# Six gather buffers and later matrix products in the three middle stages of a graph network kernel

## The reference

```
# layer 1
scale = norm(h[src]) * norm(h[dst]) + 1e-6           # norms over all edges
c     = relu((h[src] * h[dst] / scale) @ proj_cosim)
gate  = exp(clip(c.sum(-1), -5, 5))
diff  = segment_sum(h[src] - h[dst], dst)            # per node
out   = relu(segment_sum(diff[src] * gate, dst) @ W_ffn.T + b_ffn)
# layer 2
agg   = segment_sum(h[src], dst)
out   = relu((h + agg) @ W0 + b0) @ W1 + b1
```

## Time and profile before

| what | value |
|---|---|
| median of 3 runs | 5672.16 us (5667.63 to 5672.7) |
| profiled execution, span | 6105.6 us (its page gives no other time of its own) |
| PE busy | 4432.3 us (73%) |
| DVE busy | 4412.9 us (72%) |
| POOL busy | 3619.2 us (59%) |
| ACT busy | 2446.8 us (40%) |
| mean granted TensorE clock | 0.784 of full speed |

### The profile page before, as it was taken

The page is one execution under the profiler, slowest core; times in us unless marked ns, Lnnn a source line. Parts: engine busy times, 40 slices in busy tenths (PEclk is TensorE's granted clock), DMA queues, the critical chain, the costliest instruction groups (busy, mean ns, idle before and its releaser), DMA issues. The chain is left out here.

```text
span 6105.6 us, 72124 instructions
## 1 busy us (share of the span) xinstructions
PE 4432.3 (73%) x17616; PEld 2513.0 (41%) x17681; DVE 4412.9 (72%) x7837; ACT 2446.8 (40%) x7859; POOL 3619.2 (59%) x3943
## 2 busy tenths in 40 slices
PE   0577776679999986999655546555787878777776
PEld 0455554534444434666444432222333334344443
DVE  5678787768888878999766656555666766666665
ACT  0567776624434432555433322211222333333333
POOL 1556655466666640000267668776777667777776
PEclk9888898889999998999755555555778866767776
DMA  9233234433434337999533324444555522222221
GB/s 360 100 103 105 100 117 131 131 76 84 88 82 88 86 71 200 285 286 287 165 87 86 85 75 108 105 103 99 135 144 143 140 76 65 66 65 61 64 63 37
DMA packets 833422, 725.15 MB, mean 119 GB/s; under 512 B 535904, under 2 KB 543010, under 8 KB 832880
## 3 DMA queue, kind: packets, MB, share of 16 engines
q1 hardware_dynamic: 534000, 513.27, 28.9%
q0 software_dynamic: 101440, 90.01, 8.3%
q10 hardware_dynamic: 197568, 117.25, 6.2%
HBM read 450.28 MB, written 273.76 MB: 119 GB/s over the span
## 5 line engine op out<-in xcount | busy, mean ns | idle before, releaser
L1382 POOL DMA_INDIRECT df_hs<-u,keep_idx x392 | 419.1, 1069 | 879.5 <-POOLq L243 701.9
L802 POOL DMA_INDIRECT t<-keep_ptr_pay,keep_scat_ptr x392 | 410.0, 1046 | 390.6 <-DVE den_df L659 138.3
L896 POOL DMA_INDIRECT sc_xg<-t,keep_gather x392 | 435.8, 1112 | 329.3 <-DVE sc_h L196 175.2
L1382 POOL DMA_INDIRECT hd_gat<-u,keep_idx x392 | 475.5, 1213 | 158.8 <-issue 116.5
L1909 POOL DMA_INDIRECT out_x<-hd_x,keep_scat_out x392 | 453.3, 1156 | 143.3 <-issue 118.5
L1382 POOL DMA_INDIRECT ml_gat<-u,keep_idx x392 | 399.8, 1020 | 158.9 <-issue 93.5
L1382 POOL DMA_INDIRECT pr_gat<-sd,keep_idxsd x392 | 408.6, 1042 | 137.1 <-issue 69.9
L1543 PE MATMUL df_ps_p<-keep_weights,df_prod 64*128 64x64 f32 x784 | 189.8, 421 | 271.7 <-ACT df_junk_p L1526 156.4
L1065 PE MATMUL sc_ps_r<-sc_qx,keep_weights 128*64 128x512 f32 x784 | 359.4, 601 | 31.3 <-DVE sc_prod L977 28.1
L1371 PE MATMUL at_ps_m<-at_vx,keep_msg_twice 128*128 128x512 f32 x784 | 361.7, 605 | 22.6 <-DVE at_vx L1262 22.6
L2049 PE MATMUL hd_ps_h<-keep_weights,hd_xb 128*128 128x128 f32 x784 | 245.7, 413 | 145.3 <-DVE hd_wn L1992 119.9
(11 more groups left out here) (313 smaller groups left out, 12478.9 us busy)
## 6 DMA issues: line engine op xcount, KB each, us to landing
u<-den_dh SPq DMA_DIRECT2D x196, 256.0 KB
t<-tab_row ACTq DMA_DIRECT2D x98, 272.0 KB, 11.3
tab_x<-in_x SPq DMA_DIRECT2D x98, 256.0 KB
den_dx<-in_x SPq DMA_DIRECT2D x98, 256.0 KB
out_x<-den_dx SPq DMA_DIRECT2D x98, 256.0 KB
sc_et<-in_etype_row SPq DMA_DIRECT2D x98, 256.0 KB
at_v<-vt SPq DMA_DIRECT2D x196, 128.0 KB
at_et<-in_etype_row SPq DMA_DIRECT2D x98, 256.0 KB
```

Source lines behind the costliest of these rows:

```text
L802: pool.indirect_dma_start(pairs, bass.IndirectOffsetOnAxis(ap=e.scat_ptr[:, c:c + 1], axis=0), e.ptr_pay[:, c, :], None, bounds_check=NP * ...
L896: pool.indirect_dma_start(xg[i][:, u, :], None, e.T0, bass.IndirectOffsetOnAxis(ap=e.gather0[:, b.n, u:u + 1], axis=0), bounds_check=NP - ...
L1382: pool.indirect_dma_start(gat[i][:, u, :], None, table, bass.IndirectOffsetOnAxis(ap=idx_all[:, c:c + 1], axis=0), bounds_check=rows - 1, ...
```

## The change

Only `difference`, `propagate`, `mlp` and `gather` are touched. The tiles that POOL gathers into get AHEAD = 6 places, all other rings W = 5 places, each with its own semaphores. The waits that guard a place move with them: POOL may be 6 groups ahead of its reader, not 3. PSUM: `difference` has T = 4 places of ps_t (3 before), `propagate` T = 3 for ps_t and ps_x as before and two places for ps_f (one before), `mlp` two places for hid (one before). The lags between engines grow:

| stage, what | before | after |
|---|---|---|
| difference: group that DVE reads in ps_t in step n | n-1 | n-2 |
| difference: product, transposed sd on PE; their readers on ACT | n-2; n-2 | n-3; n-3 |
| propagate: PE turn, W_ffn, transpose | n-1, n-3, n-5 | n-1, n-4, n-7 |
| propagate: DVE scan, add, norm; ACT relu | n-2, n-4, n-6; n-3 | n-3, n-6, n-9; n-5 |
| mlp: PE W0, W1, transpose, last turn, own rows, gathered rows | n-2, n-2, n-4, n-6, n, n | n-3, n-5, n-7, n-9, n-1, n |
| mlp: DVE scan, x3, norm; ACT relu, copy out | n-1, n-3, n-5; n-2, n-6 | n-2, n-6, n-8; n-4, n-10 |

`ps_p`, `ps_b`, `ps_1`, `ps_2`, `ps_o`, and the ps_x and last-turn tile of mlp stay single. The memset behind each gather is gone. The order on PE changes in `difference` (the turn of hs comes first) and in `mlp`.

The core of the diff:

```diff
+AHEAD = 6
+W = 5
...
-def gather(pool, table, idx_all, gat, gathered, st, pos, rows, rest=None, rested=None):
+def gather(pool, table, idx_all, gat, gathered, st, pos, rows):
...
-        if rest is not None:
-            wait(pool, rested, st.n * TU + u)
-            pool.memset(rest[:, :], 0.0).then_inc(rested, 1)
... difference
-        hs = [s.sb(f"hs{i}", [P, TU, D]) for i in range(U)]
+        hs = [s.sb(f"hs{i}", [P, TU, D]) for i in range(AHEAD)]
...
+        T = 4
+        ps_t = [s.ps(f"t{i}", [D, GE]) for i in range(T)]
...
-                    wait(pool, turned, st.n - (U - 1), e.pool_passed)
-                    wait(pool, sq1, st.n - (U - 1), e.pool_passed)
+                    wait(pool, turned, st.n - (AHEAD - 1), e.pool_passed)
+                    wait(pool, sq1, st.n - (AHEAD - 1), e.pool_passed)
...
-                    b = st.back(1)
+                    b = st.back(2)
                     if b.on():
                         v.wait_ge(turned, b.n + 1)
                         v.wait_ge(hb_done, b.n + 1)
-                        wait(v, p_ready, b.n - (U - 1))
+                        wait(v, p_ready, b.n - (W - 1))
...
-                    b = st.back(2)
+                    b = st.back(3)
+                    if st.on():
+                        r = st.ring(AHEAD)
+                        wait(pe, gathered[r.s], 16 * TU * (r.k + 1), e.pe_passed)
+                        wait(pe, sd_done, st.n - (T - 1), e.pe_passed)
+                        for u in range(TU):
+                            m = pe.transpose(ps_t[st.n % T][:, u * P:(u + 1) * P], hs[r.s][:, u, :], e.C["ident"])
+                        m.then_inc(turned, 1)
... propagate
-        ps_f = s.ps("f", [D, GE])
+        F = 2
+        ps_f = [s.ps(f"f{i}", [D, GE]) for i in range(F)]
...
-                    b, f, g = st.back(2), st.back(4), st.back(6)
+                    b, f, g = st.back(3), st.back(6), st.back(9)
...
-                    d, f, x = st.back(1), st.back(3), st.back(5)
+                    d, f, x = st.back(1), st.back(4), st.back(7)
...
-                        wait(pe, relu_done, f.n, e.pe_passed)
-                        pe.matmul(ps_f[:, :], e.W["ffnT"][0:D, :], agg[f.s][:, :], start=True, stop=True).then_inc(f_ready, 1)
+                        wait(pe, relu_done, f.n - (F - 1), e.pe_passed)
+                        pe.matmul(ps_f[f.n % F][:, :], e.W["ffnT"][0:D, :], agg[f.s][:, :], start=True, stop=True).then_inc(f_ready, 1)
... mlp
-                    d, x, t = st.back(2), st.back(4), st.back(6)
+                    o, d, f, x, t = st.back(1), st.back(3), st.back(5), st.back(7), st.back(9)
+                    if f.on():
+                        wait(pe, hid_done, f.n + 1, e.pe_passed)
+                        wait(pe, x3_done, f.n, e.pe_passed)
+                        pe.matmul(ps_2[:, :], e.W["w1"], hid[f.n % 2][:, :], start=True, stop=True).then_inc(h2_ready, 1)
```

More of the change, by code:

```diff
@@ L35 @@
 LAST = 2
-REST = 128
 EARLY = 48
@@ L84, in first, with ring @@
         return isinstance(self.n, int) and self.n == 0
+    def ring(self, size):
+        return Step(self.n, self.n // size, self.n % size, size)
 def run_groups(eng, body, u=U, tail=LAST):
@@ L1440, in body @@
                         sp.dma_start(edge_rows(e.SD, pos(b) * GE), sdr[b.s][:, :, :]).then_inc(sd_out[b.s], 16)
-                run_groups(sp, body, U, 4)
-                for i in range(U):
-                    wait(sp, sd_out[i], 16 * len(range(i, NG, U)), e.sp_passed)
+                run_groups(sp, body, W, 5)
+                for i in range(W):
+                    wait(sp, sd_out[i], 16 * len(range(i, NG, W)), e.sp_passed)
             @block.vector
@@ L1550, in body @@
                         m.then_inc(b_ready, 1)
-                    if st.on():
-                        i = st.s
-                        wait(pe, gathered[i], 16 * TU * (st.k + 1), e.pe_passed)
-                        wait(pe, sd_done, st.n - (U - 1), e.pe_passed)
-                        for u in range(TU):
-                            m = pe.transpose(ps_t[i][:, u * P:(u + 1) * P], hs[i][:, u, :], e.C["ident"])
-                        m.then_inc(turned, 1)
-                run_groups(pe, body)
+                run_groups(pe, body, W, 3)
                 wait(pe, tot_done, 1, e.pe_passed)
@@ L1589, in body @@
                 def body(st):
-                    wait(pool, gm_done, st.n - (U - 1), e.pool_passed)
-                    gather(pool, e.SD, e.idxsd, gat, gathered, st, st.n, EP, rest, rested)
-                run_groups(pool, body, U, 0)
+                    wait(pool, gm_done, st.n - (AHEAD - 1), e.pool_passed)
+                    gather(pool, e.SD, e.idxsd, gat, gathered, st, st.n, EP)
+                run_groups(pool, body, AHEAD, 0)
             @block.sync
@@ L1608, in body @@
                         sp.dma_start(e.X2T[:, bass.ds(b.n * GE, GE)], x2[b.s][:, :]).then_inc(x2_out[b.s], 16)
-                run_groups(sp, body, U, 5)
-                for i in range(U):
-                    wait(sp, x2_out[i], 16 * len(range(i, NG, U)), e.sp_passed)
+                run_groups(sp, body, W, 7)
+                for i in range(W):
+                    wait(sp, x2_out[i], 16 * len(range(i, NG, W)), e.sp_passed)
             @block.vector
@@ L1728, in body @@
                 def body(st):
-                    wait(pool, t_ready, st.n - (U - 1), e.pool_passed)
-                    gather(pool, e.U2, e.idx2, gat, gathered, st, st.n, EP + NP, rest, rested)
-                run_groups(pool, body, U, 0)
+                    wait(pool, t_ready, st.n - (AHEAD - 1), e.pool_passed)
+                    gather(pool, e.U2, e.idx2, gat, gathered, st, st.n, EP + NP)
+                run_groups(pool, body, AHEAD, 0)
             @block.sync
@@ L1796, in body @@
                 def body(st):
-                    d, g, t = st.back(2), st.back(5), st.back(6)
-                    if t.on():
-                        a.dma_start(edge_rows(e.U3, t.n * GE), hx[t.s][:, :, 0:D]).then_inc(h_out[t.s], 16)
+                    d, g, o, t = st.back(4), st.back(8), st.back(9), st.back(10)
+                    if o.on():
+                        a.dma_start(edge_rows(e.U3, o.n * GE), hx[o.s][:, :, 0:D]).then_inc(h_out[o.s], 16)
                     if d.on():
                         a.wait_ge(h1_ready, d.n + 1)
-                        a.activation(hid[:, :], ps_1[:, :], ACT.Relu, bias=e.W["b0"]).then_inc(hid_done, 1)
+                        a.activation(hid[d.n % 2][:, :], ps_1[:, :], ACT.Relu, bias=e.W["b0"]).then_inc(hid_done, 1)
                     if t.on():
@@ L1828, in body @@
                         pe.matmul(ps_1[:, :], e.W["w0"][0:D, :], hh[d.s][:, :], start=True, stop=True).then_inc(h1_ready, 1)
+                    if x.on():
+                        wait(pe, x3_done, x.n + 1, e.pe_passed)
+                        wait(pe, x_kept, x.n, e.pe_passed)
+                        for u in range(TU):
+                            m = pe.transpose(ps_x[:, u, :], x3[x.s][:, u * P:(u + 1) * P], e.C["ident"][0:D, 0:D])
+                        m.then_inc(x_ready, 1)
                     if t.on():
@@ L1834, in body @@
                         m.then_inc(hx_turned, 1)
+                    if o.on():
+                        wait(pe, own_in[o.s], 16 * (o.k + 1), e.pe_passed)
+                        wait(pe, hh_done, o.n, e.pe_passed)
+                        for u in range(TU):
+                            m = pe.transpose(ps_o[:, u * P:(u + 1) * P], own[o.s][:, u, :], e.C["ident"])
+                        m.then_inc(o_ready, 1)
                     if st.on():
[L1836 to L1838 removed]
+                        r = st.ring(AHEAD)
+                        wait(pe, gathered[r.s], 16 * TU * (r.k + 1), e.pe_passed)
+                        wait(pe, agg_done, st.n - (T - 1), e.pe_passed)
                         for u in range(TU):
[L1840 removed]
+                            m = pe.transpose(ps_t[st.n % T][:, u * P:(u + 1) * P], gat[r.s][:, u, :], e.C["ident"])
                         m.then_inc(t_ready, 1)
[L1842 to L1858 removed]
+                run_groups(pe, body, W, 9)
 def heads(nc, e):
```

200 lines of the change are left out of this document (90 added, 110 removed).

## The result

The changed kernel took 5639.59 us (median of 4 runs, 5635.02 to 5642.8), the kernel before 5671.07 us beside it (4 runs, 5667.63 to 5672.7): a ratio of 0.9947, 95% interval 0.9933 to 0.9961, or -31 us. Forecast were 5572 us. The sign held and so did the range for 8 in 10 (5455 to 5690), but not the forecast's own range (5520 to 5620); the size was a third of what was forecast. The profiled execution took 5638.5 us, so here span and time agree; the execution read ahead of the prediction had a span of 6105.6 us against a median of 5672.16. So the span fell by 469 us and the median by 31, the sign that the prediction had named for a lateness of the profile alone.

A forecast was written before the change was run, and what follows sets the result against it. Waits between engines, mainly for late PE products, were taken to bound the three stages. Difference -15, propagate -60, mlp -50 and tails +17 gave -108 us, times 0.929 100, so 5572 us; own range 5520 to 5620, 8 in 10 5455 to 5690.

The forecast's parts named there:

- 0.929: Whole kernel: factor 5672.16/6105.6 that carries differences in the profiled span over to the median of the runs.
- only the memset: Rival, whole kernel: lateness belongs to the profiled execution, so only memsets gain, less tails; 5623 us, chance 0.22.
- Memsets: Propagate and mlp: 0.09 us for each of twice 392 memsets, 35 us a stage where others wait for POOL.
- Forecast -15: Difference: about half of ACT's 35.3 us wait for hb, the part from late turns, goes; bounds 0 and -59.
- The ring of product, transposed sd and relu sums: Difference: PE and ACT wait on each other through single ps_p and ps_b; 4.34 us a group when on time.
- SP's loads, 0: SP's loads and stores with five places: no idle time is named after their loads, so 0 us.
- The -60: Propagate: longer lags remove DVE's waits for late products, memset goes; -60 us, bounds -82 and 0.
- The -50: Mlp: W1 no longer waits in its step for ACT's relu; -50 us, half of the gain down to POOL's pace.
- The slower rival: Mlp: W0 lengthens the ring from DVE's x through x3, W1 and transpose; 5726 us, chance 0.16.
- Forecast +17: Ends of the three stages: more lag means more steps after the last gather; half of at most 33 us, +17.
- Floor: Rival, difference, propagate and mlp: all three reach POOL's pace, -207 us; 5465 us, chance 0.18.
- The change does not do what it says: Rival: products come through when POOL pauses, and POOL running further ahead pauses later; 5672 us within 0.2%, chance 0.08.

The follow-up runs named there:

- before_again: The kernel before, unchanged, profiled once more on chip 14, where products come on time: 5669.37 us.
- The wide memset: The kernel before with 512 instead of 128 elements in each memset of propagate and mlp, on chip 10: 6262.33 us, ratio 1.0184.
- the fourth run of the later store: The kernel before with difference alone changed and SP's store two steps later, on chip 12: 5666.67 us, ratio 1.0008.

## Why the prediction was wrong

**What bounds the kernel.** The failing step: it took the waits for late products of the profiled execution for waits of the kernel as timed, and carried the sum over to the runs by 0.929. They go with the chip of that execution, or its state. Of the 64, 45 and 66 us that POOL waits for others in the earlier trace rows, before_again shows nothing, with the same kernel. The parts of the sum that were to remove them, most of -15 - 60 - 50, had nothing to remove. The warning was in the numbers (a span 433.4 us above the median), and the rival *only the memset* drew the right conclusion and had 0.22. Its 5623 us were 17 too low: it had no long gathers (16.6 us), and 17 instead of 25 us of tails; its factor 0.929, for which a prompt chip has no use, gave 4 back.

**Memsets.** Right: 0.09 us each, 784 times 71 us; measured -67 (60 to 76 by the interval of its ratio). They were more than the whole gain: with the memsets kept, the rest of the change cost 44 us on the same chip.

**Difference.** Forecast -15, measured +23: +16.6 for long gathers behind SP's store, +6.7 of tail. The ring of product, transposed sd and relu sums doesn't set the pace at all on a prompt chip. The floor of 537 us was too high as well: its gather of 1.069 us on average held 90 long ones, and before_again has 1.007 and 512.6 us. Of the signs announced, the idle time ahead of DVE's product is below 60 (42.7), but PE's ahead of the projection product is not over 200 (4.9, and 41.9 ahead of its weights), and the stretch is 529, not over 570. "SP's loads, 0" was the wrong term: the load of same is now what DVE waits for, 54.4 us.

```profile
L1554 PE MATMUL df_ps_p<-keep_weights,df_prod 64*128 64x64 f32 x784 | 192.6, 424 | 4.9 <-ACT df_junk_p L1530 4.9
...
L1548 PE MATMUL df_ps_t<-keep_consts,df_hs 128*64 128x128 f32 x392 | 104.1, 421 | 214.7 <-DMA df_hs<-u,keep_idx 214.7
...
L1465 DVE SCALAR_TENSOR_TENSOR df_ps_l<-df_same,df_hd 64x512 f32<-64x512 f32 x98 | 68.2, 696 | 71.6 <-DMA df_same<-same_next 54.4 <-issue 9.5 <-DMA df_hd<-xh 7.2
...
L1458 DVE TENSOR_TENSOR df_prod<-df_ps_t,df_hb 64x512 f32<-64x512 f32 x98 | 66.3, 676 | 42.7 <-PE df_ps_t L1548 42.7
```

**Propagate.** Stretch 536, inside the 530 to 560, for the wrong reason: without the memset alone it is 535.8. The lags add nothing. On late chips, where they were to bring 25 beyond the memset, they bring 6 (622.2 to 616.0) or nothing (610.6 and 613.8), or 9 with the memset kept (602.6 to 594.0, chip 10), and the longer tails take more than that. The -60 was thus 28 in the gathers, all of it the memset's.

**Mlp.** 511.1, at POOL's floor and not at 550 to 590; before stood 44 above it and not 99. No ring of single tiles holds it. The -50 was near the 44, but 40 of these are the memset's (554.9 to 515.1 without it), so that was luck. The slower rival's ring doesn't show: DVE idles 72.8 us ahead of x, over the 69 that was its sign, but 90.7 in before_again, and POOL is unhindered. On late chips alone did lags, places and order do what was meant, 648 to 601 and 634 to 589 us, and the tails gave back 21 to 22 of it.

**Tails.** Forecast +17, measured +25 on a prompt chip, and on chip 15 +60 (18.6, 28.1, 36.4 without memset to 36.9, 46.4, 60.4). The bound of 33 held for the one, not for the other. It rested on a misreading too: 4890 is where the window of the earlier trace rows was cut, and mlp's last instruction ends at 4898.5, so its tail was 36 us and not 27.

**Floor.** All three stages do go at POOL's pace, but they did before. The clock stayed at 0.50 of full, 1.2 GHz, in two stages and rose from 0.89 to 0.92 in mlp: no gain from it.

**The change does not do what it says.** With 0.08 it had the mechanism of the late chips: products come through when POOL pauses, and a POOL that may run on pauses later. The wide memset fits the first half (a longer gap, or fewer gathers in the same time), the waits of chip 15 fit the second; neither is shown beyond that. There the kernel even got slower, which no rival gave for that reason.

## What to carry to other kernels

If the profiled execution is some per cent longer than the runs, a wait seen in it may not exist in them: first see whether the engine with the fixed work per step (here POOL, 4 x 1.3 us) would alone fill the time of the runs, and price only what lies above that. When a ring is made deeper, look at what else stands in the queues that feed it: here a store that waits, ahead of a load, moved a DVE operation onto the gathers. And what each part does may have another sign on another chip, so parts are to be compared with the kernel before on the same one.

## What the runs showed of the hardware

On three of the five numbered chips many of PE's products reach their readers late, in stages in which POOL gathers with 0.3 to 0.4 us between gathers: up to 8.5 us after the modelled end in difference and 6.8 in mlp of the execution of the earlier trace rows, and up to 19.5 us in mlp of the whole change on chip 15. In attend, without gathers, 294 of 297 recorded updates come within 0.1 us of it there. Signals between DVE and ACT don't suffer: in mlp of the whole change on chip 15 ACT's root in the norm started 0.03 to 0.04 us after the end of the DVE sum that it needs, all 98 times, while its relu started 1.62 us after the W0 product's end in the middle case (0.08 on a prompt chip). With a gap of 0.71 us between gathers, 272 of 274 and 420 of 424 recorded updates in propagate and mlp came on time. Between prompt and late chips the same kernel differs by 5 to 8.5%. Whether PE really finishes later there or its semaphore only arrives later, why chips differ, and which gap between 0.39 and 0.71 us is enough, or whether it is the gap, stays open. An indirect gather of 1.00 us takes up to 0.5 us longer when it starts within the first 0.4 us of a 64x512 DVE operation with two SBUF inputs (1.45 us in the row above); moving the operation, by the fourth run of the later store, removed 17 us of 527.
